# The layer norm of two MLP stages on ScalarE, with a bias that GpSimd forms

## The chip, the cores and the metric

The kernel runs on one core of one Trainium2 chip. A core has TensorE (matmuls, and transposes as matmuls), VectorE, ScalarE and GpSimd, each with its own queue of instructions that it works off in order; the queues meet only in semaphores. The metric is the device time of one execution in microseconds (us); the time of a kernel is the median of its runs.

## The reference, cut to what matters

Input are 64 sequences of 128 tokens with 128 channels. Three transformer layers (self attention, cross attention, MLP) and a final block are applied. The change touches the MLP of the second and third layer, which the kernel calls layers 1 and 2. For each token, with `mu` and `var` over its 128 channels:

```
def _ln(x):
    mu = jnp.mean(x, axis=-1, keepdims=True)
    var = jnp.var(x, axis=-1, keepdims=True)
    return (x - mu) * jax.lax.rsqrt(var + LN_EPS)
...
x_norm2 = modulate(_ln(x), shift_m, scale_m)
h = jax.nn.gelu(x_norm2 @ W_mlp1 + b_mlp1)
h = h @ W_mlp2 + b_mlp2
x = x + gate_m[:, None] * h
```

`modulate(t, shift, sc)` is `t * (1 + sc) + shift`, with one shift and scale per sequence and channel. The hidden width is 512.

## The kernel before

`build` runs the stages one after the other, with a barrier between them: setup, two attention stages of layer 0, its MLP, then for layers 1 and 2 a `packed_attention_layer` and `mlp_phase(nc, r, layer)`, then `refine_phase`. The tokens x stay in SBUF (`r.x`, in the profile `x_res`) for the whole kernel.

`mlp_phase` works on 16 groups of G = 4 sequences, 512 tokens each, and writes one queue for each engine. In all of them `body(g, ...)` is one group's turn and has four chunks c = 0 to 3 of 128 hidden channels. The turns are written out, with no loop at run time. `swiglu` is true for layer 0 only. The steps of one group in layers 1 and 2, with the lines of the profile:

1. VectorE: statistics (`ln_stats`, L1743), mean and variance `mv` (L1750), `vareps` = var + 1e-6 (L1753).
2. GpSimd: `rstd` = vareps to the power -0.5 (`rstd_of`, L1706), 128x4: one value for each token of four sequences.
3. VectorE: `xn` = (x - mean) * rstd (`ln_apply`, L1759), four instructions of 128x128.
4. TensorE: transposes xn into PSUM `l` (L1872). ScalarE: scale and shift give `hT` (`modulate`, L1823). VectorE splits it into a high part (cast, L1766) and a rest (L1768), as the matmuls are done in three products of rounded parts.
5. TensorE: for each chunk three matmuls into PSUM `u` (L299 to L301). ScalarE: gelu to `hid` (L1857). VectorE: high part of it (cast, L1807). The rest is subtracted by GpSimd for chunks 0 to 2 (L1734) and by VectorE for chunk 3 (L1813).
6. TensorE: three matmuls into `y` for each chunk. ScalarE: gate (`apply_gate`, L1834), four instructions. TensorE: transposes back (`mlp_r<-mlp_pg`, L1912). VectorE: adds into x (L1788).

These steps are spread over several turns. In turn g, TensorE's queue has for each chunk c the matmuls `up(g, c)`, then `down` of a chunk three places earlier; behind those of chunk 0 the transposes of xn for group g+1, behind those of chunk 1 the transposes of pg for group g-2. VectorE's queue adds into x of group g-2 at chunk 1, makes the statistics of group g+2 at chunks 0 and 1, splits hT of group g+1 at chunk 2, and, behind the cast of chunk 2, applies the layer norm of group g+2. GpSimd forms rstd of group g+2 ahead of the subtraction of chunk 1. ScalarE has a gelu in each chunk, two `modulate` instructions for group g+1 behind those of chunks 0 and 1, two gates for group g-1 behind those of chunks 2 and 3. `xn`, `rstd` and `mv` have one buffer each.

`after(engine, sem, value)` is a wait that is left out for values that are always met, `wait_ge` a wait, `then_inc` the signal at an instruction's end.

Of the kernel before, what the change touches and what calls it, by code (L numbers as in the profile page):

```python
# [33 lines left out]
G = 4  # L34
# [1604 lines left out]
def mlp_phase(nc, r, layer):  # L1639
# [13 lines left out]
    with nc.cleanup_on_exit(), ExitStack() as ctx:  # L1653
# [8 lines left out]
        def sem(name):  # L1662
            return nc.alloc_semaphore(tag + name)

        w1, w2 = sb("w1", [C, 2, W1], F32R), sb("w2", [C, 2, NC * C], F32R)
        stats, mv = sb("stats", [T, G, 6]), sb("mv", [T, G, 2])
        vareps, rstd = sb("vareps", [T, G]), sb("rstd", [T, G])
        xn, hT = sb("xn", [T, G, C]), sb("hT", [C, GT])
        hT2 = sb("hT2", [C, 2, 2, GT], F32R)
        half = sb("half", [C, 2, GT]) if swiglu else None  # L1670
# [7 lines left out]
        s_xT, s_hT, s_hhi, s_hlo, s_pg, s_pgps, s_x = (  # L1678
            sem(n) for n in ("xT", "hT", "hhi", "hlo", "pg", "pgps", "x"))
        s_w, s_zeroed = sem("w"), sem("zeroed")  # L1680

        s_up, s_half, s_hid, s_hi, s_lo, s_down = (sem(n) for n in ("up", "half", "hid", "hi", "lo", "down"))
        block = ctx.enter_context(nc.Block())
# [18 lines left out]
        @block.gpsimd  # L1702
        def _(pool):
            def rstd_of(g):
                pool.wait_ge(s_var, g + 1)
                nc.gpsimd.tensor_tensor(rstd[:, :], vareps[:, :], r.neg_half[:, :], ALU.pow).then_inc(s_rstd, 1)  # L1706

            def prologue():
                rstd_of(0)
                rstd_of(1)  # L1710
                if layer == 0:

                    nc.gpsimd.memset(r.zero[:, :, :], 0.0).then_inc(s_zeroed, 1)
                    nc.gpsimd.memset(r.slab[:, :], 0.0).then_inc(s_zeroed, 1)
                    for q in range(2 * 4):
                        pool.wait_ge(s_zeroed, 2 + q)
                        nc.gpsimd.affine_select(
                            out=r.slab[:, :], in_=r.slab[:, :], compare_op=ALU.not_equal, fill=1.0,
                            base=-(16 * q + 3), pattern=[[-4, 4]], channel_multiplier=1).then_inc(s_zeroed, 1)
                    pool.wait_ge(s_zeroed, 10)  # L1720
                    for buf in range(3):
                        nc.gpsimd.tensor_copy(
                            r.kp[:, buf, :, :], r.slab[:, :].rearrange("c (g k) -> c g k", k=1).broadcast_to([C, 4, GT])
                            ).then_inc(s_zeroed, 1)

            def body(g, par, late, work, add, nxt, nxt2):
                for c in range(NC if work else 0):
                    n = NC * g + c
                    if c == 1 and nxt2:
                        rstd_of(g + 2)  # L1730
                    if swiglu or c < NC - 1:
                        pool.wait_ge(s_hi, n + 1)

                        nc.gpsimd.tensor_tensor(hid2[:, c, 1, :], hid[:, c % NB, :], hid2[:, c, 0, :].bitcast(F32),  # L1734
                                                ALU.subtract).then_inc(s_lo, 1)

            iterations(pool, body, prologue)

        @block.vector
        def _(dve):  # L1740
# [4 lines left out]
                    last.then_inc(s_stats, 1)  # L1745

            def ln_variance(g):
                after_alone(dve, s_stats, g + 1)
                for b in range(G):
                    last = nc.vector.bn_aggr(mv[:, b, :], stats[:, b, :])  # L1750
# [2 lines left out]
                nc.vector.tensor_scalar(vareps[:, :], mv[:, :, 1], 1e-6, None, ALU.add).then_inc(s_var, 1)  # L1753

            def ln_apply(g):
                after(dve, s_xT, g)
                dve.wait_ge(s_rstd, g + 1)
                for b in range(G):
# [57 lines left out]

        @block.scalar
        def _(act):
            def modulate(g, bs):
                after(act, s_hlo, g)  # L1820
                after_alone(act, s_xT, g + 1)
# [19 lines left out]
            def body(g, par, late, work, add, nxt, nxt2):  # L1841
                for c in range(NC):
# [17 lines left out]
                        modulate(g + 1, [2 * c, 2 * c + 1])  # L1860
                    if c >= 2 and late:
                        apply_gate(g - 1, 1 - par, [2 * c - 4, 2 * c - 3])

            iterations(act, body, lambda: modulate(0, range(G)))

        @block.tensor
        def _(pe):
# [726 lines left out]
```

## Time and profile before

| | us |
|---|---|
| median of 3 runs | 3640.77 (3635.32 to 3642.21) |
| the profiled execution | 3631.1 |
| its span, first to last instruction | 3629.3 |
| MLP of layer 1 in it, about | 2215.9 to 2364.8 |
| MLP of layer 2 in it, about | 3071.1 to 3220.2 |

The profile is of one execution. Its page gives busy times of the engines over the span; the other views used here are the timeline (instructions in order of time, neighbours of one kind merged), groups of instructions by line, and a table of busy times in a stretch. `PE` is TensorE, `PEld` its weight loads, `DVE` VectorE, `ACT` ScalarE, `POOL` GpSimd. Names such as `mlp_xn<-x_res` say what is written and read, without the number of the layer. Times within the profile are set against its own 3631.1 us, which lies 0.27% below the median.

### The profile page before, as it was taken

The numbers are of one execution on the slowest core, as the hardware profiler recorded it, in microseconds if no ns is written. First come the engines' busy times: TensorE is split into PE (matmuls) and PEld (weight loads), VectorE is DVE, ScalarE is ACT, GpSimd is POOL, SyncE is SP. The second block draws the span as 40 slices with busy tenths as digits, with TensorE's granted clock in tenths as the row PEclk, the third lists the DMA queues.
The fourth block names the chain that finished last, engine by engine and source line by source line (L and its number), as shares of the span: only waits on it lengthen the run. The fifth ranks groups of instructions, "written<-read, shape, count | busy, mean of one in ns | idle before, by whom it ended". The sixth has DMA issues, their size and how long they took to land. (4 is left out here: it accounts for less than half of the span.)

```text
span 3629.3 us, 94366 instructions
## 1 busy us (share of the span) xinstructions
PE 3103.4 (86%) x31983; PEld 2065.1 (57%) x31983; DVE 2810.7 (77%) x12664; ACT 2171.0 (60%) x5124; POOL 1200.7 (33%) x1534
## 2 busy tenths in 40 slices
PE   3999967777777769789999997879999998879999
PEld 2454534444444437556666664646666665558887
DVE  5677759999999978578887766858887774966665
ACT  1566645555555647557776665637776664646665
POOL 2000026666666656521122213531112211532221
PEclk9999978889888879889999987969999996979999
DMA  4000000000000000034444430024444441000000
GB/s 130 12 13 13 13 9 8 8 8 9 6 8 8 6 2 1 21 97 107 106 106 104 105 82 3 1 76 106 106 108 100 104 104 29 1 23 10 13 13 16
DMA packets 135426, 162.87 MB, mean 45 GB/s; under 512 B 40742, under 2 KB 85414, under 8 KB 134566
## 3 DMA queue, kind: packets, MB, share of 16 engines
q1 hardware_dynamic: 114182, 121.62, 13.5%
q0 software_dynamic: 12160, 26.04, 3.1%
q10 hardware_dynamic: 8608, 9.18, 1.0%
q8 instruction: 261, 4.28, 0.5%
q14 instruction: 215, 1.76, 0.2%
HBM read 13.81 MB, written 4.19 MB: 5 GB/s over the span
## 5 line engine op out<-in xcount | busy, mean ns | idle before, releaser
L1253 ACT ACTIVATE attn_pT<-attn_t 128x512 f32<-128x512 f32 (+1 forms) x1024 | 555.5, 596 | 335.4 <-PE attn_t L1509 334.6
L1370 DVE TENSOR_REDUCE attn_mx<-attn_s 128x4 f32<-128x512 f32 (+1 forms) x1024 | 549.6, 579 | 152.8 <-PE attn_s L1494 151.3
L636 ACT ACTIVATE topk_prob<-topk_s,topk_nmx 128x77 f32<-128x77 f32 x1024 | 248.3, 326 | 319.7 <-POOL topk_nmx L532 213.2
L1494 PEld LDWEIGHTS attn_s<-packed_keys,packed_queries 32*128 32x128 f32 x4096 | 282.9, 193 | 164.1 <-DVE attn_mx L1370 97.1
L1175 POOL DMA_DIRECT2D packed_queries<-attn_om x256 | 142.7, 557 | 662.9 <-ACT attn_om L1246 659.2
L1494 PE MATMUL attn_s<-packed_keys,packed_queries 32*128 32x128 f32 (+1 forms) x4096 | 348.4, 291 | 14.3 <-DVE attn_mx L1370 6.2
L1534 PE MATMUL attn_o<-attn_pT,attn_vp 128*18 128x128 f32 (+1 forms) x8192 | 336.5, 284 | 0.0
L538 POOL TENSOR_SCALAR topk_mask<-topk_work 128x308 f32<-128x308 f32 x256 | 252.9, 988 | 224.5 <-DVE topk_work L779 222.5
L1509 PE MATMUL attn_t<-packed_queries,packed_keys 32*128 32x128 f32 (+1 forms) x4096 | 306.0, 268 | 1.8 <-ACT attn_pT L1253 1.8
L927 PE MATMUL topk_t<-ident,topk_prob 128*77 128x128 f32 x1024 | 187.3, 313 | 138.5 <-POOL topk_prob L542 138.1
L927 PEld LDWEIGHTS topk_t<-ident,topk_prob 128*77 128x77 f32 x1024 | 139.7, 171 | 250.3 <-issue 140.7
L917 PE MATMUL topk_s<-kbd,topk_qT 128*128 128x308 f32 x512 | 220.9, 517 | 47.4 <-ACT topk_prob L636 43.3
L1734 POOL TENSOR_TENSOR mlp_hid<-mlp_hid 128x512 fp32r<-128x512 f32 x160 | 209.7, 1311 | 156.1 <-DVE mlp_hid L1807 107.9
L1509 PEld LDWEIGHTS attn_t<-packed_queries,packed_keys 32*128 32x128 f32 (+1 forms) x4096 | 232.5, 169 | 6.8 <-ACT attn_pT L1253 4.4
L774 DVE MATCH_REPLACE8 topk_work<-topk_top,topk_s 128x77 f32<-128x77 f32 x1024 | 222.9, 235 | 0.0
L1534 PEld LDWEIGHTS attn_o<-attn_pT,attn_vp 128*18 128x18 f32 (+1 forms) x8192 | 185.2, 99 | 64.5 <-issue 46.2
L542 POOL TENSOR_TENSOR topk_prob<-topk_prob,topk_mask 128x308 f32<-128x308 f32 x256 | 213.5, 834 | 21.3
L779 DVE MATCH_REPLACE8 topk_work<-topk_top,topk_work 128x77 f32<-128x77 f32 x1024 | 218.3, 231 | 0.0
L1554 PE MATMUL attn_l<-packed_keys 128*128 128x512 f32 x576 | 209.0, 454 | 0.8 <-DVE attn_vp L1360 0.7
L763 DVE MAX8 topk_top<-topk_s 128x8 f32<-128x77 f32 x1024 | 172.7, 235 | 23.0 <-PE topk_s L917 23.0
L768 DVE MAX8 topk_top<-topk_work 128x8 f32<-128x77 f32 x1024 | 165.8, 228 | 0.0
L1171 POOL TENSOR_TENSOR attn_rstd<-attn_vareps,neg_half 128x4 f32<-128x4 f32 x64 | 65.8, 1029 | 293.4 <-DVE attn_vareps L1328 293.3
(309 smaller groups left out, 7780.0 us busy)
## 6 DMA issues: line engine op xcount, KB each, us to landing
packed_queries<-attn_qT SPq DMA_DIRECT2D x720, 64.0 KB, 2.2
packed_keys<-attn_kT SPq DMA_DIRECT2D x384, 64.0 KB, 2.1
packed_queries<-attn_om POOLq DMA_DIRECT2D x256, 64.0 KB, 2.4
packed_queries<-zero_rows SPq DMA_DIRECT2D x120, 128.0 KB, 2.7
packed_keys<-attn_kT SPq DMA_DIRECT2D x384, 39.0 KB, 2.1
kbd<-window_kT SPq DMA_DIRECT2D x512, 8.0 KB
kbd<-topk_kT SPq DMA_DIRECT2D x512, 4.8 KB
weights<-in_weights ACTq DMA_DIRECT2D x1, 3524.5 KB, 14.6
```

The source lines that it names most:

```text
L538: nc.gpsimd.tensor_scalar(mask[:, u % 2, :], work[:, u % 4, :], NEG / 2, None, ALU.is_le).then_inc(s_mask, 1)
L542: nc.gpsimd.tensor_tensor(prob[:, u % 4, :], prob[:, u % 4, :], mask[:, u % 2, :], ALU.mult).then_inc(s_picked, 1)
L636: last = nc.scalar.activation(prob[:, u % 4, h * keys:(h + 1) * keys], s_ps[:, u % 2, h * keys:(h + 1) * keys], ACT.Exp, scale=SCALE, bias ...
L774: last = nc.vector.match_replace(wk_[u % 4][:, h, :], top[:, u % 2, h, :], sc[:, h, :], NEG)
L779: last = nc.vector.match_replace(wk_[c % 4][:, h, :], top2[:, c % 2, h, :], wk_[c % 4][:, h, :], NEG)
L917: last = nc.tensor.matmul(s_ps[:, u % 2, 0:cols], qT[:, par, b * T:(b + 1) * T], r.kbd[:, HU * g:HU * g + HU, b * keys:(b + 1) * keys], st ...
L927: last = nc.tensor.transpose(t_ps[0:rows, c % 2, j * T:(j + 1) * T], prob[:, c % 4, j * rows:(j + 1) * rows], r.ident[:, :])
L1253: nc.scalar.activation(pT[0:keys, c % 2, h, :], t_ps[0:keys, h, :], ACT.Exp, scale=SCALE).then_inc(s_exp, 1)
L1370: nc.vector.tensor_reduce(mx[:, (c // 2) % 2, 2 * k + h, :], sc, AX.X, ALU.max).then_inc(s_max, 1)
L1494: last = nc.tensor.matmul(s_ps[:, h, k * KW:(k + 1) * KW], r.qp[32 * j:32 * j + 32, buf, k, b * T:(b + 1) * T], r.kp[32 * j:32 * j + 32, b ...
L1509: last = nc.tensor.matmul(t_ps[0:keys, h, k * T:(k + 1) * T], r.kp[32 * j:32 * j + 32, buf, k, b * KW:b * KW + keys], r.qp[32 * j:32 * j + ...
L1534: last = nc.tensor.matmul(o_ps[32 * k:32 * k + 18, v * T:(v + 1) * T], vp[0:keys, buf, b, k, v, a, :], pT[0:keys, c % 2, a, k * T:(k + 1) ...
```

## The change

In layers 1 and 2, `xn` is formed by ScalarE as `Identity(rstd * x + nmr)`, with `nmr` = -mean * rstd, one value for each token. GpSimd forms nmr with two more 128x4 instructions behind the power, the second of which waits for the first. VectorE's four instructions of L1759 are gone; layer 0 stays as it was. On ScalarE two of the four stand behind the gates of chunk 2 and two behind those of chunk 3, for group g+2. Three waits protect the single buffers: rstd is not overwritten before the last xn that reads it is done, mv not before nmr is formed, xn not before it is transposed.

```
+        nmr = None if swiglu else sb("nmr", [T, G])
...
+        s_nmr = sem("nmr")
...
         @block.gpsimd
         def _(pool):
             def rstd_of(g):
+                if not swiglu:
+                    after(pool, s_xn, g)
                 pool.wait_ge(s_var, g + 1)
                 nc.gpsimd.tensor_tensor(rstd[:, :], vareps[:, :], r.neg_half[:, :], ALU.pow).then_inc(s_rstd, 1)
+                if not swiglu:
+                    pool.wait_ge(s_rstd, g + 1)
+                    nc.gpsimd.tensor_tensor(nmr[:, :], mv[:, :, 0], rstd[:, :], ALU.mult).then_inc(s_nmr, 1)
+                    pool.wait_ge(s_nmr, 2 * g + 1)
+                    nc.gpsimd.tensor_scalar(nmr[:, :], nmr[:, :], -1.0, None, ALU.mult).then_inc(s_nmr, 1)
...
             def ln_variance(g):
+                if not swiglu:
+                    after(dve, s_nmr, 2 * g)
                 after_alone(dve, s_stats, g + 1)
...
             def ln_apply(g):
+                if not swiglu:
+                    return
                 after(dve, s_xT, g)
...
         @block.scalar
         def _(act):
+            def ln_apply(g, bs):
+                if swiglu:
+                    return
+                if bs[0] == 0:
+                    after(act, s_xT, g)
+                    act.wait_ge(s_nmr, 2 * g + 2)
+                for b in bs:
+                    last = nc.scalar.activation(xn[:, b:b + 1, :], r.x[:, G * g + b:G * g + b + 1, :], ACT.Identity,
+                                                scale=rstd[:, b:b + 1], bias=nmr[:, b:b + 1])
+                if bs[-1] == G - 1:
+                    last.then_inc(s_xn, 1)
+
...
                     if c >= 2 and late:
                         apply_gate(g - 1, 1 - par, [2 * c - 4, 2 * c - 3])
-
-            iterations(act, body, lambda: modulate(0, range(G)))
+                    if c >= 2 and nxt2:
+                        ln_apply(g + 2, [2 * c - 4, 2 * c - 3])
+
+            def prologue():
+                ln_apply(0, range(G))
+                modulate(0, range(G))
+                ln_apply(1, range(G))
+
+            iterations(act, body, prologue)
```

The order of the instructions on ScalarE, layer 1, chunks 2, 3 and 0 of one turn and the next, before (L1857 is the gelu, L1834 the gate, L1823 scale and shift):

```order
L1857 ACTIVATE mlp1_hid<-mlp1_u,bias_cols 128x512
L1834 ACTIVATE mlp1_pg<-mlp1_y,gate_bias,mod 128x128 x2
L1857 ACTIVATE mlp1_hid<-mlp1_u,bias_cols 128x512
L1834 ACTIVATE mlp1_pg<-mlp1_y,gate_bias,mod 128x128 x2
L1857 ACTIVATE mlp1_hid<-mlp1_u,bias_cols 128x512
L1823 ACTIVATE mlp1_hT<-mlp1_l,mod 128x128 x2
```

And after, where L1883 is the gelu, L1860 the gate, L1849 scale and shift:

```order
L1883 ACTIVATE mlp1_hid<-mlp1_u,bias_cols 128x512
L1860 ACTIVATE mlp1_pg<-mlp1_y,gate_bias,mod 128x128 x2
L1840 ACTIVATE mlp1_xn<-x_res,mlp1_nmr,mlp1_rstd 128x128 x2
L1883 ACTIVATE mlp1_hid<-mlp1_u,bias_cols 128x512
L1860 ACTIVATE mlp1_pg<-mlp1_y,gate_bias,mod 128x128 x2
L1840 ACTIVATE mlp1_xn<-x_res,mlp1_nmr,mlp1_rstd 128x128 x2
L1883 ACTIVATE mlp1_hid<-mlp1_u,bias_cols 128x512
L1849 ACTIVATE mlp1_hT<-mlp1_l,mod 128x128 x2
```

Between the first and the last xn of a group (L1840) stand a gelu and two gates.

VectorE, layer 1, from the statistics to the rest of chunk 3, before:

```order
L1750 BN_AGGR mlp1_mv<-mlp1_stats 128x2 x4
L1753 TENSOR_SCALAR mlp1_vareps<-mlp1_mv 128x4
L1807 CAST mlp1_hid2<-mlp1_hid 128x512
L1766 CAST mlp1_hT2<-mlp1_hT 128x512
L1768 TENSOR_TENSOR mlp1_hT2<-mlp1_hT,mlp1_hT2 128x512
L1807 CAST mlp1_hid2<-mlp1_hid 128x512
L1759 TENSOR_SCALAR mlp1_xn<-x_res,mlp1_mv,mlp1_rstd 128x128 x4
L1807 CAST mlp1_hid2<-mlp1_hid 128x512
L1813 TENSOR_TENSOR mlp1_hid2<-mlp1_hid,mlp1_hid2 128x512
```

After:

```order
L1762 BN_AGGR mlp1_mv<-mlp1_stats 128x2 x4
L1765 TENSOR_SCALAR mlp1_vareps<-mlp1_mv 128x4
L1821 CAST mlp1_hid2<-mlp1_hid 128x512
L1780 CAST mlp1_hT2<-mlp1_hT 128x512
L1782 TENSOR_TENSOR mlp1_hT2<-mlp1_hT,mlp1_hT2 128x512
L1821 CAST mlp1_hid2<-mlp1_hid 128x512 x2
L1827 TENSOR_TENSOR mlp1_hid2<-mlp1_hid,mlp1_hid2 128x512
```

The four instructions between the casts of chunks 2 and 3 are gone; nothing else moved there.

## Rows read from the trace of the kernel before

**Rows 1.** The page, part 1: busy us (share of the span) and instructions.

```profile
PE 3103.4 (86%) x31983; PEld 2065.1 (57%) x31983; DVE 2810.7 (77%) x12664; ACT 2171.0 (60%) x5124; POOL 1200.7 (33%) x1534
```

**Rows 2.** Busy us by stretch: ten groups of the MLP of layer 1.

```profile
core 0: us, PE busy (x) PEld busy (x) DVE busy (x) ACT busy (x) POOL busy (x), PEclk, DMA share, GB/s
2258.00:2344.44 86.44, 70.88 (x322) 50.61 (x321) 80.63 (x212) 55.60 (x121) 50.59 (x41) 1.00 0.00 1
```

**Rows 3.** Timeline, TensorE: start us, us, line, [idle before, releaser].

```profile
2268.59 0.63 PE L1872 MATMUL mlp_l<-ident,mlp_xn 128*128 128x128 f32 x4 [1.40 <-DVE mlp_xn L1759]
...
2277.24 0.63 PE L1872 MATMUL mlp_l<-ident,mlp_xn 128*128 128x128 f32 x4 [1.39 <-DVE mlp_xn L1759]
```

**Rows 4.** Timeline, VectorE in that group, and L1759 eight groups on.

```profile
2271.10 0.69 DVE L1788 TENSOR_TENSOR x_res<-mlp_r,x_res 128x512 f32<-128x512 f32 x1 [0.48 <-PE mlp_r L1912]
...
2272.53 0.42 DVE L1766 CAST mlp_hT<-mlp_hT 128x512 fp32r<-128x512 f32 x1
2272.98 0.69 DVE L1768 TENSOR_TENSOR mlp_hT<-mlp_hT 128x512 fp32r<-128x512 f32 x1
2273.59 1.52 DVE L1807 CAST mlp_hid<-mlp_hid 128x512 fp32r<-128x512 f32 x1
2275.03 2.06 DVE L1759 TENSOR_SCALAR mlp_xn<-x_res,mlp_mv,mlp_rstd 128x128 f32<-128x128 f32 x4
...
2344.16 2.06 DVE L1759 TENSOR_SCALAR mlp_xn<-x_res,mlp_mv,mlp_rstd 128x128 f32<-128x128 f32 x4
```

**Rows 5.** Timeline, start of the MLP of layer 1.

```profile
2218.68 1.11 DVE L1759 TENSOR_SCALAR mlp_xn<-x_res,mlp_mv,mlp_rstd 128x128 f32<-128x128 f32 x4 [0.20 <-POOL mlp_rstd L1706]
...
2219.85 1.12 PE L1872 MATMUL mlp_l<-ident,mlp_xn 128*128 128x128 f32 x4 [5.65 <-DVE mlp_xn L1759]
...
2221.00 1.50 ACT L1823 ACTIVATE mlp_hT<-mlp_l,mod 128x128 f32<-128x128 f32 x4 [7.97 <-PE mlp_l L1872]
...
2222.49 1.12 DVE L1759 TENSOR_SCALAR mlp_xn<-x_res,mlp_mv,mlp_rstd 128x128 f32<-128x128 f32 x4 [0.25 <-POOL mlp_rstd L1706]
...
2223.52 0.42 DVE L1766 CAST mlp_hT<-mlp_hT 128x512 fp32r<-128x512 f32 x1
```

**Rows 6.** Timeline, GpSimd in the group of rows 3.

```profile
2272.36 1.12 POOL L1706 TENSOR_TENSOR mlp_rstd<-mlp_vareps,neg_half 128x4 f32<-128x4 f32 x1 [0.38 <-DVE mlp_vareps L1753]
2273.45 1.37 POOL L1734 TENSOR_TENSOR mlp_hid<-mlp_hid 128x512 fp32r<-128x512 f32 x1
2275.19 1.31 POOL L1734 TENSOR_TENSOR mlp_hid<-mlp_hid 128x512 fp32r<-128x512 f32 x1 [0.36 <-DVE mlp_hid L1807]
```

**Rows 7.** Small GpSimd instructions of other stages: two groups (busy, mean ns), then timeline.

```profile
L532 POOL TENSOR_SCALAR topk_nmx<-topk_top 128x4 f32<-128x4 f32 x256 | 58.1, 227 | 41.6 <-DVE topk_top L763 20.5
...
L2054 POOL TENSOR_TENSOR refine_w1s<-refine_weights,refine_w1s 128x256 fp32r<-128x256 f32 x1 | 0.7, 722 | 0.0
...
1519.95 1.01 POOL L1171 TENSOR_TENSOR attn_rstd<-attn_vareps,neg_half 128x4 f32<-128x4 f32 x1 [1.62 <-DVE attn_vareps L1328]
...
800.24 0.98 POOL L538 TENSOR_SCALAR topk_mask<-topk_work 128x308 f32<-128x308 f32 x1 [0.61 <-DVE topk_work L779]
801.30 0.84 POOL L542 TENSOR_TENSOR topk_prob<-topk_prob,topk_mask 128x308 f32<-128x308 f32 x1
802.22 0.23 POOL L532 TENSOR_SCALAR topk_nmx<-topk_top 128x4 f32<-128x4 f32 x1
802.57 0.33 ACT L636 ACTIVATE topk_prob<-topk_s,topk_nmx 128x77 f32<-128x77 f32 x1 [1.24 <-POOL topk_nmx L532]
```

**Rows 8.** Timeline, ScalarE in the group of rows 3.

```profile
2272.56 0.81 ACT L1834 ACTIVATE mlp_pg<-mlp_y,gate_bias,mod 128x128 f32<-128x128 f32 x2
2273.26 0.69 ACT L1857 ACTIVATE mlp_hid<-mlp_u,bias_cols 128x512 f32<-128x512 f32 x1
2273.85 0.80 ACT L1834 ACTIVATE mlp_pg<-mlp_y,gate_bias,mod 128x128 f32<-128x128 f32 x2
```

**Rows 9.** Timeline, end of the MLP of layer 1, ScalarE to TensorE.

```profile
2361.83 1.50 ACT L1834 ACTIVATE mlp_pg<-mlp_y,gate_bias,mod 128x128 f32<-128x128 f32 x4 [2.74 <-PE mlp_y L301]
...
2363.48 0.63 PE L1912 MATMUL mlp_r<-ident,mlp_pg 128*128 128x128 f32 x4 [1.75 <-ACT mlp_pg L1834]
```

## The prediction, made before the changed kernel ran

> **What bounds the kernel now.** Read the page first. No engine is at its limit over the whole span: TensorE is busy 86%, VectorE 77%, ScalarE 60%, GpSimd 33% [rows 1]. The page averages over eight stages, and the change touches two of them, the MLP of layer 1 and of layer 2, about 150 us each. So the next view is the table of busy time over a stretch of the layer 1 MLP that holds ten groups: 86.44 us, of which TensorE is busy 70.88, VectorE 80.63, ScalarE 55.60 and GpSimd 50.59, at a granted clock of 1.00 [rows 2]. VectorE looks like the bound, but its busy time holds waiting.
>
> The timeline shows what closes the loop. One group takes 8.65 us, from one block of L1872 transposes (xn to PSUM) to the next, 2268.59 to 2277.24, and before the second the TensorE sat idle 1.39 us for L1759 on VectorE [rows 3]. I follow that period back.
> - From the transposes at 2268.59, TensorE goes on through six matmuls, the transposes of pg, and VectorE can add into x at 2271.10 (L1788): **2.51 us** [rows 3, 4].
> - From there VectorE is busy without a gap to the end of L1759, 2275.03 + 2.06 = 2277.09: **5.99 us** [rows 4].
> - VectorE's end to the next transposes: 2277.24 - 2277.09 = **0.15 us**.
>
> The sum, 2.51 + 5.99 + 0.15 = 8.65, is the period. L1759 starts at 2275.03 and again, eight groups on, at 2344.16 [rows 4], 8.64 us each. Two rows of it are swollen: the cast L1807 takes 1.52 us where L1766, a cast of the same shape, takes 0.42, and the four L1759 take 2.06 us against 1.11 to 1.12 at the start of the stage [rows 4, 5]. Both run while GpSimd's subtractions L1734 run (2273.45 + 1.37 = 2274.82; the next begins at 2275.19) [rows 4, 6].
>
> **What the change removes from the loop.** The four L1759 (2.06 us) go, and so does VectorE's part of the loop behind the small statistics: nothing of the next xn waits any more for L1766, L1768 and the blocked L1807. What stays of the 5.99 us is L1788 to the start of GpSimd's pow L1706: 2272.36 - 2271.10 = 1.26 us. The rest, 5.99 - 1.26 = 4.73 us, is replaced.
>
> **What it puts in.** Now xn depends on pow, multiply, negate (GpSimd), then on ScalarE. In order:
> - pow, as before: 1.12 us [rows 6]. Until now it lay beside VectorE's work; now it is in the loop.
> - multiply, 128x4, tensor by tensor: no such row exists. Below: GpSimd's 128x512 takes 1.31 us and its 128x256 takes 0.72 us [rows 6, 7], 0.59 us for 256 columns, so a line through them leaves 0.14 us for four columns. Above: pow itself has this shape and takes 1.01 us when VectorE leaves it alone [rows 7]. I take 0.20, near the line and near the 0.23 us of a GpSimd TENSOR_SCALAR of 128x4 [rows 7], since a multiply is what the wide rows are made of and a power is not.
> - negate: 0.23 us, that same row.
> - two gaps, as each of the two waits for the end of the one before: L542 waits for L538 in that way and starts 801.30 - 801.22 = 0.08 us behind it [rows 7]. I take 0.10 each.
> - GpSimd to ScalarE: 802.57 - 802.45 = 0.12 us [rows 7].
> - ScalarE's stretch from the first to the last xn. The new order there is two xn, gelu, two gates, two xn (the order rows of the change). Two L1834 hold ScalarE for 2273.26 - 2272.56 = 0.70 us, so 0.35 each, and a gelu for 2273.85 - 2273.26 = 0.59 us, while the last one counts whole, 0.46 us [rows 8]. Sum: 5 x 0.35 + 0.59 + 0.46 = 2.80 us.
> - ScalarE to TensorE: 2363.48 - (2361.83 + 1.50) = 0.15 us [rows 9].
>
> The new loop: 2.51 + 1.26 + 1.12 + (0.10 + 0.20 + 0.10 + 0.23) + 0.12 + 2.80 + 0.15 = **8.59 us** against 8.65. So 3.6 us of saved and unblocked VectorE work buys 0.06 us per group: the gain is handed to a chain of the same length on other engines. The three prices in the brackets have 0.63 us; the period is as before when they have 0.69.
>
> Is anything else late before that? ScalarE's load rises by 4 x 0.35 us, from 5.5 busy to about 7 of 8.6: not the bound, but its gelu of chunk 3 now stands behind two xn that wait for GpSimd. That gelu would start at 2273.48 + 0.63 + 0.12 + 0.70 = 2274.93 instead of 2273.26 [rows 8]; it feeds the cast of chunk 3, L1813 and matmuls that stand behind the next transposes and add, so I cost it at nothing. The subtraction L1734 of chunk 1 stands on GpSimd behind the two new instructions, 0.63 us later; the matmuls of L299 that wait for it end a microsecond before the transposes (TensorE's idle 1.39 us [rows 3] is the cover), so nothing either, as long as the bracket stays under about 1.5 us. The added waits that only protect a buffer (s_xn on GpSimd, s_nmr on VectorE, s_xT on ScalarE) were met a whole half-group before.
>
> **The start of each stage.** Before, the first transposes are at 2219.85; the ScalarE part ends at 2221.00 + 1.50 = 2222.50, but the cast L1766 waits until 2223.52, behind the second L1759 [rows 5]. The first L1759 starts at 2218.68, 0.03 us behind pow, and 2219.85 - 2218.65 = 1.20 us pass from pow to the transposes. After, they are 0.63 + 0.12 + (3 x 0.35 + 0.46) + 0.15 = 2.41 us, 1.2 us later. The wait behind L1759 hid 1.0 of that, so 0.2 us is lost, 0.4 us in both layers. The second xn on ScalarE and the table load behind it fit before the first gelu.
>
> **The sum.** Twelve full periods in each layer: 24 x (8.59 - 8.65) = -1.4 us; start +0.4 us; total -1.0 us. The profiled execution took 3631.1 us (span 3629.3), so it would be 3630.1. The median of the runs shown is 3640.8, 0.27% above it; a change of one microsecond moves both alike: **3639.8 us**. A measurement of this kernel can tell about 0.2%, 7.3 us, from no change; that is 0.30 us per group over 24 groups, so everything between periods of 8.35 and 8.95 us reads as the same.
>
> **The rivals.**
> *Slower, the read port.* In the loop the multiply would start at 2273.48 + 0.10 = 2273.58. VectorE's L1768 runs until 2273.67 and the cast L1807 would run from 2273.59 to 2274.01, now unblocked [rows 4, 6]. If GpSimd's small operations can read only when VectorE is through with both, the multiply ends near 2274.2 and the negate near 2274.5, a bracket of 1.0 us: period 8.96, 24 x 0.31 + 0.4 = +7.8 us, **3648.6 us**. It is slower from a bracket of 0.69 us on. For it: pow takes 1.12 us here and 1.01 us where VectorE is idle [rows 6, 7], and VectorE's own cast was held until GpSimd ended. Against it: pow lost only 0.11 us although three VectorE instructions passed beside it, and they lost nothing [rows 4, 6]. The Trainium skill, SBUF — State Buffer, "Who interferes with whom", says that a cast in the two-port mode and GpSimd exclude each other for the whole instruction, whoever issues first, and that a VectorE instruction with two SBUF inputs keeps out GpSimd's reads. By that rule this rival is the likely one if the cast is issued first, and the 1.52 us cast agrees; the pow row speaks for short conflicts only.
>
> *Slower, dearer pieces.* The multiply costs like pow, 1.01 us: period 9.40, +18 us + 0.4, **3659 us**. Or an xn on ScalarE, reading SBUF instead of PSUM with two pointer operands, takes up its whole 0.46 us without overlap: three intervals, +0.33 us, period 8.92, +6.9 us, 3647.7 us. For PSUM sources the rows show the overlap; for this source none does.
> By the Trainium skill, ScalarE: Activation LUTs, "What ACT_TABLE_LOAD costs", an ACTIVATE has a fixed cost, 0.093 us for each pointer operand and 0.833 ns per element, and back to back they overlap; worked out, an estimate, 0.39 us apart instead of the 0.35 us of the rows [rows 8]. With three xn intervals the loop would be 0.12 us longer. The rows decide, and its result stays within no change.
>
> *Faster, cheap pieces.* Multiply 0.14 as on the line, negate 0.20 and gaps of 0.06 make the bracket 0.46 us and the period 8.42: 24 x (-0.23) + 0.4 = -5.1 us, 3635.7 us. With 0.33 instead of 0.35 us between ScalarE's instructions it is 8.32, -7.5 us, **3633.3 us**. A larger gain needs xn to leave the loop altogether; TensorE's busy time would then allow 7.1 us and less. The in-order queue of TensorE, in which the transposes stand before the matmuls that the next add into x needs, forbids it.
>
> **How the numbers follow.** Forecast, period 8.42 to 8.85: 0.66. The port: 0.17. Dearer pieces: 0.06. Cheap pieces: 0.11. The port rival lies right at the bound, so I count three quarters of it as slower; with the dearer pieces that is 0.19. The cheap case reaches 7.3 us only at its far end; with the scatter of the runs and an error of my chain itself I count 0.09 as faster. Same: 0.72. The range takes in the cheap end and the port rival with a microsecond of scatter, 3633 to 3650, and leaves out the dear multiply and the tails.
>
> **What would show it.** In the profile after: L1840 (the four xn on ScalarE) as what TensorE's transposes wait for, in place of L1759; the period between blocks of transposes within 0.2 us of 8.65; ScalarE idle before the first xn of a group, ended by GpSimd's negate; the two GpSimd instructions at 0.2 us each; the cast at 0.42 us in chunk 2, where it now stands as L1821 and meets no subtraction (the one of chunk 3 may be the blocked one instead, at no cost); VectorE's busy time in the stretch of ten groups down from 80.6 us by the ten times 2.06 of L1759, to about 60. I am wrong if the multiply or the negate is much over 0.3 us, if the xn on ScalarE are more than 0.4 us apart, or if the transposes wait for something that is no part of this chain.

## Result, and the profile after

| | before | after |
|---|---|---|
| median, us | 3639.03 (3634.42 to 3642.21, 5 runs) | 3654.18 (3649.85 to 3663.13, 5 runs) |
| profiled execution, us | 3631.1 | 3649.85 |

The ratio is 1.0053, 95% interval [1.0032, 1.0075]. I forecast no change, 3639.8 us with a range to 3650; the kernel became slower by about 15 us (12 to 27 us by the interval). Times and ratios below leave out two executions, one of e9 (5060 us) and one of e16 (4350 us), in which the granted clock was 0.66 and 0.64 instead of about 0.92 over the whole execution.

The page of after, part 1, beside [rows 1]:

```profile
PE 3115.8 (85%) x31983; PEld 2072.8 (57%) x31983; DVE 2742.8 (75%) x12536; ACT 2221.2 (61%) x5252; POOL 1217.0 (33%) x1598
```

VectorE gave up 68 us and ScalarE took on 50 us, as meant. Ten groups of the layer 1 MLP of after, busy us by stretch, columns as in [rows 2]:

```profile
2246.76:2340.82 94.06, 75.40 (x321) 54.10 (x320) 57.60 (x171) 70.75 (x160) 55.50 (x60) 0.95 0.00 1
```

Three things stand there. Ten groups take 94.06 us instead of 86.44. VectorE's busy time is down from 80.63 to 57.60, close to the 60 that I expected. And the granted clock reads 0.95, where before it was 1.00: something that the prediction does not speak of.

The starts of GpSimd's pow (L1706 before, L1711 after; 16 in each stage) give every period. Before, the eleven from the fifth pow on are all 8.63 to 8.65 us in layer 1. After, in layer 1: 8.92, 8.93, 8.94, **10.51**, 8.94, 8.93, 8.93, **10.53**, **10.50**, 8.93, 8.93, 8.94; in layer 2 five of twelve are 10.4 to 10.7. So there are two losses: 0.28 us in every group, and 1.5 to 1.8 us more in eight of the 24. Here is one ordinary group, timeline of after (start us, us, engine, line, [idle before, releaser]):

```profile
2284.62 0.69 DVE L1782 TENSOR_TENSOR mlp_hT<-mlp_hT 128x512 fp32r<-128x512 f32 x1
2285.23 0.48 POOL L1714 TENSOR_TENSOR mlp_nmr<-mlp_mv,mlp_rstd 128x4 f32<-128x4 f32 x1
2285.23 0.42 DVE L1821 CAST mlp_hid<-mlp_hid 128x512 fp32r<-128x512 f32 x1
2285.80 0.23 POOL L1716 TENSOR_SCALAR mlp_nmr<-mlp_nmr 128x4 f32<-128x4 f32 x1
2286.12 0.88 ACT L1840 ACTIVATE mlp_xn<-x_res,mlp_nmr,mlp_rstd 128x128 f32<-128x128 f32 x2 [1.11 <-POOL mlp_nmr L1716]
2287.31 0.50 PE L299 MATMUL mlp_y<-mlp_hid,mlp_w 128*128 128x512 f32 x1 [0.96 <-POOL mlp_hid L1744]
2288.16 0.87 ACT L1840 ACTIVATE mlp_xn<-x_res,mlp_nmr,mlp_rstd 128x128 f32<-128x128 f32 x2
2289.17 0.63 PE L1905 MATMUL mlp_l<-ident,mlp_xn 128*128 128x128 f32 x4 [0.91 <-ACT mlp_xn L1840]
2291.68 0.69 DVE L1802 TENSOR_TENSOR x_res<-mlp_r,x_res 128x512 f32<-128x512 f32 x1 [1.06 <-PE mlp_r L1945]
2292.69 0.17 DVE L1765 TENSOR_SCALAR mlp_vareps<-mlp_mv 128x4 f32<-128x4 f32 x1
2293.00 1.09 POOL L1711 TENSOR_TENSOR mlp_rstd<-mlp_vareps,neg_half 128x4 f32<-128x4 f32 x1 [1.03 <-DVE mlp_vareps L1765]
```

The loop is the one of the prediction: the transposes L1905 (in place of L1872, [rows 3]) wait for ScalarE's L1840, ScalarE for the negate L1716, GpSimd for vareps, VectorE for the transposes of pg. The multiply L1714, however, takes 0.48 us and starts in the same hundredth as VectorE's cast L1821. At the start of the stage, where no cast of this kind stands beside it, the same instruction takes 0.20 us (timeline of after, GpSimd; the negate behind it takes 0.25):

```profile
2227.79 0.20 POOL L1714 TENSOR_TENSOR mlp_nmr<-mlp_mv,mlp_rstd 128x4 f32<-128x4 f32 x1
```

The long groups are another matter. Stretches of after in layer 1 (columns as above, so the granted clock is the third number from the end):

```profile
2310.00:2315.00 5.00, 4.04 (x16) 2.48 (x14) 2.92 (x11) 3.58 (x9) 3.97 (x5) 1.00 0.00 0
2315.00:2320.00 5.00, 4.11 (x16) 3.37 (x16) 2.38 (x7) 3.60 (x9) 1.58 (x2) 0.66 0.00 0
2320.00:2325.00 5.00, 4.04 (x18) 2.74 (x17) 2.86 (x11) 3.06 (x7) 3.45 (x5) 1.00 0.00 0
```

and TensorE's own timeline in the second of them and just behind it:

```profile
2315.98 0.84 PE L1905 MATMUL mlp_l<-ident,mlp_xn 128*128 128x128 f32 x4 [0.89 <-ACT mlp_xn L1840]
2317.05 0.63 PE L300 MATMUL mlp_u<-mlp_hT,mlp_w 128*128 128x512 f32 x1
2317.48 0.63 PE L301 MATMUL mlp_u<-mlp_hT,mlp_w 128*128 128x512 f32 x1
...
2320.09 0.39 PE L300 MATMUL mlp_u<-mlp_hT,mlp_w 128*128 128x512 f32 x1
2320.32 0.40 PE L301 MATMUL mlp_u<-mlp_hT,mlp_w 128*128 128x512 f32 x1
```

From the transposes on, matmuls start 0.43 us apart (2317.05 to 2317.48); three microseconds later it is 0.23 again (2320.09 to 2320.32). In between TensorE works at the lower level of its clock, 1.2 GHz, for some four microseconds; the 0.66 of the stretch is a mean of 1.00 and 0.50. In both kernels the stage begins at the lower level, as the stage ahead of it ended (granted clock 0.50 until about 2228 before and 2238 after). From there to the last group the kernel before stays at 1.00.

Where the time went: between the first and the last pow the two stages grew by 132.11 - 123.98 = 8.1 and 135.17 - 124.23 = 10.9 us, 19.1 together. The eight low-clock groups hold 12.8 of these, the longer period nearly all of the rest (24 x 0.28 = 6.7). Ahead of the two stretches, between them and behind them the two profiled executions differ by +9.1, -10.3 and +0.6 us, which add up to nearly nothing. So the profiled executions differ by 19 us, the medians by 15.

### The profile page after: what moved, and what is told of

Same layout as the page of the kernel before. It is cut to its first block and busy times, and to the rows that moved or that the text cites. A ratio compares the mean times of both kernels' runs of the same rounds, so it can differ in the third digit from the quotient of the medians.

```text
span 3647.8 us, 94490 instructions
## 1 busy us (share of the span) xinstructions
PE 3115.8 (85%) x31983; PEld 2072.8 (57%) x31983; DVE 2742.8 (75%) x12536; ACT 2221.2 (61%) x5252; POOL 1217.0 (33%) x1598
## 5 line engine op out<-in xcount | busy, mean ns | idle before, releaser
L622 ACT COPY topk_pT<-topk_t 77x512 f32<-77x512 f32 x256 | 150.3, 587 | 26.8 <-PE topk_t L927 26.2
```

## Experiments

Periods below are the usual distances between the starts of pow at full clock, from the fifth on. The low-clock groups are counted in one profiled execution of each kernel, of 24 groups in the two stages. Each kernel was run beside the kernel before on its own chip, and ratios are against that. The chips differ: the kernel before had medians of 3631.26 us beside e1, e3, e4 and e5, 3634.33 beside e2, e8, e9 and e10, and 3631.02 beside e12, e15 and e16, against 3639.03 in the table above. So kernels are compared by their ratios and not by their microseconds.

| run | period, us | low-clock groups | ratio to before |
|---|---|---|---|
| before | 8.65 | 0 | 1 |
| after | 8.93 | 8 | 1.0053 [1.0032, 1.0075] |
| e1 cast behind multiply | 8.94 | 14 | 1.0074 [1.0061, 1.0088] |
| e8 cast behind negate | 8.65 | 0 | 1.0010 [0.9996, 1.0024] |
| e2 negate first | 8.88 | 11 | 1.0052 [1.0033, 1.0072] |
| e3 six filler matmuls | 8.93 | 0 | 1.0015 [1.0003, 1.0027] |
| e15 three, first gap | 8.93 | 0 | 1.0011 [0.9991, 1.0030] |
| e16 three, second gap | 8.93 | 0 | 1.0013 [0.9999, 1.0028] |
| e4 before, four aggregations | 8.89 | 0 | 1.0020 [1.0005, 1.0034] |
| e9 before, eight | 9.15 | 0 (e9b) | 1.0039 [1.0022, 1.0055] |
| e5 early variance | 8.41 | 1 | 0.9988 [0.9978, 0.9998] |
| e10 before, early variance | 8.85 | 0 | 1.0014 [0.9996, 1.0032] |
| e12 variance in chunk 0 | 8.71 | about 10 | 1.0013 [0.9998, 1.0028] |

### The multiply and the cast

```
                         dve.wait_ge(s_hid, n + 1)
+                        if c == 2 and nxt2:
+                            dve.wait_ge(s_nmr, 2 * (g + 2) + 1)
                         nc.vector.tensor_copy(hid2[:, c, 0, :], hid[:, c % NB, :]).then_inc(s_hi, 1)
```

> After, with one added wait on VectorE: the cast L1821 of chunk 2, which starts in the same moment as GpSimd's multiply, now waits until the multiply has ended. Nothing else is moved. Theory one (the multiply takes 0.48 us and not 0.20 because the cast runs beside it): the multiply falls to 0.20 us, the negate stays at 0.23 if the cast no longer meets a small instruction, and the period at full clock goes from 8.93 to 8.93 - 0.28 = 8.65 us; 24 x (-0.28) = -6.7 us, 3647.5 us if the clock drops stay. Rival (the multiply is slow for itself, for instance behind a pow): it stays at 0.48 us and the period at 8.93 us, 3654 us. Third way: the conflict moves on to the negate, which then takes about 0.48 us, and nothing is gained.

Measured: 3657.19 us, and the third way. One group of that run, timeline:

```profile
2299.89 0.20 POOL L1714 TENSOR_TENSOR mlp_nmr<-mlp_mv,mlp_rstd 128x4 f32<-128x4 f32 x1
2300.18 0.51 POOL L1716 TENSOR_SCALAR mlp_nmr<-mlp_nmr 128x4 f32<-128x4 f32 x1
2300.22 0.43 DVE L1823 CAST mlp_hid<-mlp_hid 128x512 fp32r<-128x512 f32 x1 [0.25 <-PE mlp_y L301]
```

The multiply is back to 0.20 us, and the negate behind it, which had taken 0.23, takes 0.51. Whichever small instruction stands beside the cast is held for about 0.28 us; that it is "slow for itself" is excluded. The multiply still begins beside the end of VectorE's L1782 in this run and takes its 0.20 us, so in after it was the cast that held it. So the next run took the cast out of both, the same edit with `2 * (g + 2) + 2`:

> As the run with the cast behind the multiply, where the conflict only moved on to the negate (0.51 us beside the cast, and the multiply down to 0.20), but now the cast of chunk 2 waits for the negate too. Theory: both small instructions run alone, 0.20 and 0.23 us, and the period falls from 8.93 by 0.28 to 8.65 us; against the after kernel -6.7 us and fewer groups at the low clock, 3636 to 3648 us. Rival: the cast is now issued together with GpSimd's subtraction of chunk 1 and one of them is held for the other's whole length, about 1.3 us; if the subtraction is the one held, TensorE's matmul L299 that waits for it (0.96 us idle) becomes later, and the period stays or grows: 8.9 to 9.2 us, 3655 us or more.

Measured: 3638.90 us, timeline of one group:

```profile
2282.52 0.20 POOL L1714 TENSOR_TENSOR mlp_nmr<-mlp_mv,mlp_rstd 128x4 f32<-128x4 f32 x1
2282.81 0.23 POOL L1716 TENSOR_SCALAR mlp_nmr<-mlp_nmr 128x4 f32<-128x4 f32 x1
2283.00 1.28 POOL L1744 TENSOR_TENSOR mlp_hid<-mlp_hid 128x512 fp32r<-128x512 f32 x1
2283.13 0.88 ACT L1842 ACTIVATE mlp_xn<-x_res,mlp_nmr,mlp_rstd 128x128 f32<-128x128 f32 x2 [0.84 <-POOL mlp_nmr L1716]
2283.17 3.03 DVE L1823 CAST mlp_hid<-mlp_hid 128x512 fp32r<-128x512 f32 x2 [0.56 <-POOL mlp_nmr L1716]
2284.33 0.51 PE L299 MATMUL mlp_y<-mlp_hid,mlp_w 128*128 128x512 f32 x1 [0.68 <-POOL mlp_hid L1744]
2286.19 0.63 PE L1907 MATMUL mlp_l<-ident,mlp_xn 128*128 128x128 f32 x4 [0.88 <-ACT mlp_xn L1842]
```

The cast starts 0.17 us behind the subtraction, and now it is VectorE that is held: two casts in 3.03 us, each of them beside a subtraction. Nobody waits for them in this loop; the matmul L299 comes earlier, not later (idle 0.68 instead of 0.96). The period is 8.65 us, and the low-clock groups are gone with it. With this one wait the changed kernel does what I had predicted for the change alone: its ratio to before is 1.0010, no change.

The negation was also moved out of the chain to the front, as a negated mean that GpSimd forms before pow (`nm = -mv`, then pow, then `nmr = nm * rstd`):

> After, with GpSimd's negation moved out of the chain: it negates the mean as soon as the aggregation is there, beside VectorE's vareps, and ahead of pow; behind pow only the multiply is left. Removed from the chain are the negate and its gap, 0.23 + 0.09 = 0.32 us; pow starts later by what the negate (0.23 us) outlasts vareps (0.17 us) and a gap, some 0.15 us. Theory (the chain through GpSimd and ScalarE closes the loop): the period goes from 8.93 to about 8.93 - 0.32 + 0.15 = 8.76 us, -4 us, and fewer groups at the low clock, between 3636 and 3650 us. Rival (the loop closes elsewhere): 8.93 us stays.

Measured: 3658.07 us, period 8.88, timeline:

```profile
2281.99 0.43 DVE L1825 CAST mlp_hid<-mlp_hid 128x512 fp32r<-128x512 f32 x1
2282.06 0.73 POOL L1714 TENSOR_SCALAR mlp_nm<-mlp_mv 128x4 f32<-128x4 f32 x1 [0.87 <-DVE mlp_mv L1766]
2282.33 0.42 DVE L1784 CAST mlp_hT<-mlp_hT 128x512 fp32r<-128x512 f32 x1
2282.47 1.38 POOL L1716 TENSOR_TENSOR mlp_rstd<-mlp_vareps,neg_half 128x4 f32<-128x4 f32 x1
2283.93 0.20 POOL L1720 TENSOR_TENSOR mlp_nmr<-mlp_nm,mlp_rstd 128x4 f32<-128x4 f32 x1
```

A miss: the negate now meets two casts and takes 0.73 us. Pow is listed from 2282.47, while the negate runs to 2282.79, so its 1.38 us hold 0.3 us of the same waiting. Of the 0.17 us that I expected 0.05 came, and the clock still falls in 11 groups.

### The clock

Six matmuls a group, whose product is overwritten, in TensorE's two gaps of after (behind the up product of chunk 0, and before the transposes):

```
+            def filler(g, par):
+                pe.wait_ge(s_hT, g + 1)
+                for _ in range(3):
+                    nc.tensor.matmul(l_ps[:, :], w1[:, 0, 0:C], hT2[:, par, 0, :], start=True, stop=True)
...
                     if work:
                         up(g, c, par)
+                    if c == 0 and nxt and work and late and not swiglu:
+                        filler(g, par)
...
                     if c == 0 and nxt and work:
+                        if late and not swiglu:
+                            filler(g, par)
                         transpose_xn(g + 1)
```

> After, with six matmuls more in every group of layers 1 and 2 that compute nothing of use (a product into the PSUM tile of xn's transposes, which overwrite it): three in the gap before the first matmul of the second-last down product, three in the gap before the transposes of xn. Both gaps are idle time of TensorE, 0.96 and 0.91 us, and three matmuls take 3 x 0.23 = 0.70 us, so they should delay nothing. Theory one (the drops of the granted clock in the two stages, nine groups of about 10.5 us instead of 8.93, come with TensorE's idle time in the longer loop, and cost 9 x 1.6 = 14 us by themselves): no five-microsecond window of the two stages under 0.95, all periods at 8.93 us or a little more, 3654 - 14 = 3640 us. Rival (the drops have nothing to do with what TensorE does in these gaps): they stay, 3654 us or more.

Measured: 3636.13 us, every period from the fifth pow on 8.93 to 8.95 us except for 8.77 and 9.21 in layer 2. (The expectation counts nine low-clock groups in after; between the first and the last pow there are eight.) A stretch of layer 1 (TensorE, its weight loads, VectorE, ScalarE, GpSimd, granted clock); layer 2 reads 1.00 as well:

```profile
2240.00:2300.00 60.00, 56.92 (x254) 41.54 (x253) 38.98 (x116) 47.66 (x109) 38.55 (x42) 1.00 0.00 1
```

TensorE does more and the kernel is faster: the distance to after, 1.0053 to 1.0015, is 0.38% or 14 us (between 5 and 23 us with both intervals), all from the clock, since the period did not move. The traces say it more closely: its stages (first to last pow) take 127.4 and 127.5 us, against 132.1 and 135.2 of after, which is 12.3 us. Then only one of the two gaps was filled:

> After, with three idle matmuls in each group instead of six, in the gap before the down product (L299, 0.96 us idle), so that 0.3 us of it is left, and the gap of 0.91 us before the transposes stays: 1.14 us idle a group in all. Theory (the low clock needs both gaps, since before has one of 1.40 us and never drops): all groups at 8.93 us, as with six, 3636 to 3641 us. Rival (either gap alone is enough): groups of 10.5 us remain, about half as many.

> The mirror of the run with three matmuls in the first gap: three in the gap before the transposes of xn (0.91 us idle, 0.2 us left), and the gap of 0.96 us before the down product stays. Theory (the low clock needs both gaps): all groups at 8.93 us, 3636 to 3641 us. Rival: groups of 10.5 us remain.

Measured: 3634.12 and 3636.17 us; all groups are at full clock in both. Three matmuls in either gap are enough. The gaps left, timeline of TensorE, first e15, then e16:

```profile
2282.11 0.50 PE L299 MATMUL mlp_y<-mlp_hid,mlp_w 128*128 128x512 f32 x1 [0.29 <-POOL mlp_hid L1744]
2283.95 0.63 PE L1905 MATMUL mlp_l<-ident,mlp_xn 128*128 128x128 f32 x4 [0.87 <-ACT mlp_xn L1840]
```

```profile
2280.45 0.50 PE L299 MATMUL mlp_y<-mlp_hid,mlp_w 128*128 128x512 f32 x1 [0.96 <-POOL mlp_hid L1744]
2282.32 0.63 PE L1905 MATMUL mlp_l<-ident,mlp_xn 128*128 128x128 f32 x4 [0.20 <-ACT mlp_xn L1840]
```

Is it simply that a longer loop leaves TensorE too idle? Then before, made longer, must drop too. Four more aggregations on VectorE, into a spare tile, then eight:

```
+                if not swiglu:
+                    for b in range(G):
+                        nc.vector.bn_aggr(spare[:, b, :], stats[:, b, :])
                 for b in range(G):
                     last = nc.vector.bn_aggr(mv[:, b, :], stats[:, b, :])
```

> The kernel before, with four more of VectorE's aggregations (L1750 of before) in each group of layers 1 and 2, written to a spare tile, between the add into x and vareps. They lengthen the loop of before by 0.30 us (four of them stand 0.40 us apart from the next row, the last counted whole), so the period goes from 8.65 to 8.95 us, about that of after, with nothing of the change in it. Theory one (the clock drops come with a loop of this length, in which TensorE is idle more): drops like those of after, 24 x 0.30 + 14 = +21 us, 3660 us. Rival (the drops belong to the changed order of work and not to the length of the loop): the clock stays at 1.00 in the two stages, +7.2 us, 3646 us.

> The kernel before, with eight more of VectorE's aggregations in each group instead of four; four of them gave a period of 8.89 us, 0.25 us over 8.65, and the clock stayed at 1.00. So the period here is 8.65 + 0.50 = 9.15 us, longer than that of after at full clock (8.93), and TensorE idles more than there: 9.15 - 7.09 = 2.06 us a group against 1.84. Theory one (the drops come with the sum of TensorE's idle time, and the run with four was just short of it): low-clock groups appear, before + 12 + up to 14 us. Theory two (they come with the way in which after spreads its idle time, 0.96 and 0.91 us two microseconds apart, where before has one gap of 1.40 us): none appear, before + 12 us.

> The same kernel as the one with eight more aggregations, looked at once more, since the profiled execution of that run was a disturbed one. The period should be 9.15 us again in all groups. If the drops of the granted clock come with the sum of TensorE's idle time, windows with a low clock appear among groups 3 to 14; if not, all windows read 1.00.

Measured: 3639.94, 3652.1 and 3645.26 us (the last is one execution). The granted clock is 1.00 in e4, and in e9b from the third group to the last of both stages. A stretch of e9b in layer 1, and TensorE's gaps in one of its groups:

```profile
2240.00:2300.00 60.00, 47.37 (x211) 1.00 0.00 1
```

```profile
2279.70 0.47 PE L299 MATMUL mlp_u<-mlp_hT,mlp_w 128*128 128x512 f32 x1 [0.49 <-ACT mlp_hid L1861]
2280.79 0.50 PE L299 MATMUL mlp_y<-mlp_hid,mlp_w 128*128 128x512 f32 x1 [0.17 <-POOL mlp_hid L1735]
2283.15 0.63 PE L1876 MATMUL mlp_l<-ident,mlp_xn 128*128 128x128 f32 x4 [1.40 <-DVE mlp_xn L1763]
```

With a period of 9.15 us, longer than that of after, and 2.06 us of idle time against 1.87, no group drops; the loss is the plain 24 x 0.5 = 12 us, within its interval (8 to 20 us). The sum of idle time is not the cause. What the traces list beside it is where the idle time lies. After, e1 and e2 each have two gaps of 0.8 to 1.05 us within two microseconds of each other, and drop. Where one of the two is filled (e3, e15, e16), or the first is 0.68 us (e8), nothing drops, and nothing drops with one gap of 1.40 us and the small ones further off (before, e4, e9b). e12, below, drops right behind single gaps of 2 us, and e5 drops once, in the one group in which its second gap was 1.18 us instead of 0.90 (timelines of e12 and of e5):

```profile
2279.43 0.47 PE L299 MATMUL mlp_y<-mlp_hid,mlp_w 128*128 128x512 f32 x1 [2.04 <-POOL mlp_hid L1744]
...
2282.47 1.05 PE L1905 MATMUL mlp_l<-ident,mlp_xn 128*128 128x128 f32 x4
```

```profile
3173.52 0.50 PE L299 MATMUL mlp_y<-mlp_hid,mlp_w 128*128 128x512 f32 x1 [0.60 <-POOL mlp_hid L1744]
3175.66 0.74 PE L1907 MATMUL mlp_l<-ident,mlp_xn 128*128 128x128 f32 x4 [1.18 <-ACT mlp_xn L1842]
```

The pattern is narrow, though, and no rule. e10, below, has gaps of 1.19 and 0.75 us in nearly every group, 2.4 us apart and 1.94 us together, more than after has, and never drops (timeline):

```profile
2282.26 0.47 PE L299 MATMUL mlp_u<-mlp_hT,mlp_w 128*128 128x512 f32 x1 [1.19 <-issue]
2284.65 0.52 PE L1874 MATMUL mlp_l<-ident,mlp_xn 128*128 128x128 f32 x3 [0.75 <-DVE mlp_xn L1759]
```

One group of e8 has 0.69 and 1.16 us (ahead of the matmuls at 3182.96 and 3185.09 us), together more than the group of e5 that drops and as far apart, and keeps its clock. What is shown is that filling either gap of after keeps the clock, and that a longer loop by itself doesn't lose it. That idle time close together is what costs it is argued from the list, and no run tests it by moving a gap alone. By the Trainium skill, TensorE: Matmul & The Clock Gate, "A second HAM failure mode: psum-queue depth-cycling", frequent short idling between groups of matmuls can make the clock swing between its two levels. The traces agree: in after the granted clock reads 1.00 and 0.66 by turns with no gap over 0.96 us in such a group of layer 1. Why eight groups of after drop and sixteen with nearly the same gaps don't stays open.

### The variance ahead of the add

In after the statistics of a later group stand behind the add into x, although they don't need it. Moved ahead of it:

```
+                    if work and nxt2 and c == 1 and not swiglu:
+                        ln_variance(g + 2)
                     if add and c == 1:
                         after_alone(dve, s_pgps, g - 1)
...
-                    if nxt2 and c == 1:
+                    if nxt2 and c == 1 and swiglu:
                         ln_variance(g + 2)
```

> After, with VectorE's variance of the group after next (aggregation and vareps) moved ahead of its add into x, so that pow, multiply and negate no longer stand behind the transposes of pg. In the trace of after vareps could be ready at 2291.1 instead of 2292.86, GpSimd's subtraction of chunk 0 ends at 2291.97, so pow would start at about 2292.0 instead of 2293.0, a microsecond earlier; ScalarE waited 1.11 us for the negate before its first xn. Theory one (the loop runs through this chain): the period falls by 0.6 to 1.0 us, to 7.9 to 8.3, and with it the clock drops go, since TensorE idles less: 3654 - 24 x 0.6 - 14 = 3625 us or less. Rival (the chain is not what closes the loop, or VectorE's later work becomes late instead): the period stays within 0.1 of 8.93, 3652 to 3656 us.

Measured: 3626.86 us, period 8.41, one low-clock group: 0.12% under before (interval 0.02 to 0.22%), 0.65% under after. The period fell short of the 7.9 to 8.3 us that I expected. Rows of its trace show what may be a part of it, timeline:

```profile
2282.44 0.69 DVE L1782 TENSOR_TENSOR mlp_hT<-mlp_hT 128x512 fp32r<-128x512 f32 x1
2282.53 0.67 POOL L1714 TENSOR_TENSOR mlp_nmr<-mlp_mv,mlp_rstd 128x4 f32<-128x4 f32 x1
```

The multiply now starts 0.09 us behind VectorE's subtraction of two SBUF tiles and ends 0.07 us behind its end: 0.67 us instead of 0.20, in 23 of 24 groups. No run takes that meeting away. The same move in the kernel before:

> The kernel before, with the same move that took 27 us off after: the variance of the group after next ahead of the add into x. Theory (the move pays only once xn has left VectorE): the aggregation fills 0.37 us of the 0.48 us in which VectorE waits for the transposes of pg, but vareps then meets GpSimd's subtraction of chunk 0 and is held until that ends, as in the after kernel with the move (1.07 us instead of 0.17), and the add starts about 0.9 us later; the other VectorE work of the loop still stands behind it. Period 8.65 - 0.48 + 0.9 = 9.07 us, +10 us against before. Rival (the move is good by itself): the period falls by up to 0.48 us to 8.17, -11 us.

Measured: 3635.96 us, period 8.85 instead of 8.65. The add starts 3.33 us behind the transposes instead of 2.51, so it loses 0.82 of the 0.9 us; from there to the end of xn it is 5.37 instead of 5.99 us, where I had counted on 0.48 us less. The held row is as foreseen in both kernels, here e5 and then e10, timeline:

```profile
2279.83 1.28 POOL L1744 TENSOR_TENSOR mlp_hid<-mlp_hid 128x512 fp32r<-128x512 f32 x1 [2.20 <-DVE mlp_hid L1823]
2280.08 1.07 DVE L1765 TENSOR_SCALAR mlp_vareps<-mlp_mv 128x4 f32<-128x4 f32 x1
2281.29 1.16 POOL L1711 TENSOR_TENSOR mlp_rstd<-mlp_vareps,neg_half 128x4 f32<-128x4 f32 x1 [0.17 <-DVE mlp_vareps L1765]
```

```profile
2287.00 1.07 DVE L1753 TENSOR_SCALAR mlp_vareps<-mlp_mv 128x4 f32<-128x4 f32 x1
```

VectorE's vareps takes 1.07 us instead of 0.17 beside the subtraction in both. In e5 the period falls all the same, as xn has left VectorE; in e10 it grows. One step further, with variance and pow in chunk 0:

> After, with the variance of the group after next directly behind its statistics in chunk 0 (in the earlier run it stood in chunk 1, behind the cast of chunk 0), and with GpSimd's pow, multiply and negate ahead of its subtraction of chunk 0 instead of that of chunk 1. In the trace of the earlier run the statistics end at 2279.42, so vareps would end at 2279.9, before GpSimd has a subtraction that could hold it (1.07 us there), and pow would start at 2279.97 instead of 2281.29; multiply and negate end near 2281.9, the first xn can follow ScalarE's gate at 2283.05 without its wait of 0.58 us. Theory: the period falls by up to that wait, from 8.41 to 7.83 us, 24 x (-0.58) = -14 us against 3627, 3613 us. Rival: GpSimd's three subtractions, now all behind the small instructions, become late for TensorE or hold VectorE's casts, and the period stays within 0.1 of 8.41, 3625 to 3629 us.

Measured: 3638.62 us, period 8.71 and, in most of the low-clock groups, 9.46 or more: a miss for both theories. GpSimd's subtractions became late, and TensorE waits for them in one piece of about 2 us, the one shown above: in 90 us of that run (groups by line) the down product L299 has 12.1 us of idle time in front of it.

```profile
L299 PE MATMUL mlp_y<-mlp_hid,mlp_w 128*128 128x512 f32 x40 | 17.5, 437 | 12.1 <-POOL mlp_hid L1744 12.1
```

## Why the prediction was wrong

Two steps failed. The granted clock was taken to stay at 1.00, and the later subtraction of chunk 1 was costed at nothing: the clock took 12.8 of the 19.1 us by which the two stages grew. And the bracket of multiply, negate and their gaps was taken at 0.63 us where it measured 0.88: with ScalarE's stretch, 0.11 us too short in the sum, it makes the period 8.93 us, and that is nearly all of the rest. With the longer period and the clock kept (e3, e15, e16) the ratio is 1.0011 to 1.0015, some 5 us, so it was the clock that took the time out of my range.

- **The loop was right.** Transposes, pg, add, vareps, pow, multiply, negate, ScalarE, transposes: each releaser in the group above is the one named. The sum with after's rows is 2.51 (2289.17 to 2291.68) + 1.32 (to pow at 2293.00) + 1.08 + 0.88 (bracket) + 0.10 + 2.91 (2286.12 to 2288.16 + 0.87) + 0.14 = 8.94 us, against 8.93 measured.
- **The bracket was mis-sized, 0.88 us instead of 0.63.** Both prices, 0.20 and 0.23 us, were right where nothing of VectorE stands beside them (e8), and the gaps were 0.08 and 0.09 us; the step that failed was to take them undisturbed. A multiply much over 0.3 us is one of the signs of being wrong that I had named. I had seen the cast standing where the multiply would start, and gave that 17 in 100 because pow loses only 0.11 us in such company. The row that spoke for it was the other one, the cast held for a whole subtraction [rows 4]. The rival put the bracket at 1.0 us, the period at 8.96 and the time at 3648.6 us; its mechanism came true for the cast, a little smaller (0.88, 8.93), and the price of the clock was in no rival. By the Trainium skill, SBUF — State Buffer, "Who interferes with whom", such a cast and GpSimd exclude each other whoever comes first, and the order of issue decides who waits. Both sides can be held, as e1 and e8 show, 0.51 instead of 0.23 us for the negate and 3.03 us for two casts. The order is less plain: in e8 the instruction listed first went through, but in e1 the negate that was held is listed 0.04 us ahead of the cast, so starts this close do not tell it.
- **ScalarE's stretch was 2.91 instead of 2.80 us.** Two xn take 0.88 us and the second of a pair starts 0.39 to 0.40 us behind the first, not 0.35 as for PSUM sources [rows 8]. The estimate worked out from the Trainium skill, ScalarE: Activation LUTs, "What ACT_TABLE_LOAD costs", was 0.39. The trace agrees, with 0.39 to 0.40. I had let the PSUM rows decide.
- **The clock was missing altogether**, 12.8 us in the traces, two thirds of what the stages lost. I read 1.00 in [rows 2] and took it as given. A longer loop alone did not change it (e4, e9b); what changed is that the wait of 0.16 us for GpSimd's subtraction became 0.96 us, since the subtraction of chunk 1 stands behind the two small instructions. I costed that delay at nothing, because TensorE's idle time covers it. It does cover it, but one gap of 1.40 us became two, 0.96 and 0.91 us. With either of the two filled the clock stays (e15, e16); why some groups drop and others don't is open.
- **The casts and buffers were right.** The chunk 2 cast takes 0.42 us again, the one of chunk 3 is the held one, VectorE's load fell as computed, and no protecting wait shows up in the full turns (GpSimd's second pow of each stage waits for the first xn, but stands 3.52 us behind the first pow where it was 3.76 before).
- **The start of a stage was right.** From pow's end to the first transposes it is 2.36 us (2227.71 to 2230.07) against my 2.41.
- **A slip without effect.** The "3.6 us of saved and unblocked VectorE work" counts the whole cast. Unblocked are 1.52 - 0.42 = 1.10 us, so it is 3.2 us; the sum doesn't use it.
- **e8 bears out the sum**: with the conflict removed, the period is 8.65 against my 8.59, most of the rest is ScalarE's stretch, and the clock stays.

## What to carry to other kernels

When small instructions of GpSimd are put into a loop's chain, look which VectorE instructions stand at that moment. In these runs such a meeting cost one of the two up to the other's remaining time, and one wait that let the cast go later was cheaper than the meeting. When a change moves or splits an idle gap of TensorE, ask what its clock will do even if nothing is late; a few idle matmuls in one gap are a cheap test of it. Taking work off an engine can need a second edit to pay: here the work moved off VectorE was worth 0.12% once the statistics had been moved ahead of the add, while that second edit alone was worth nothing in the kernel before (1.0014).

## What I had not expected of the hardware

- In layer 1 of after the granted clock fell to 1.2 GHz for about four microseconds at a time, with no gap over 0.96 us in the loop, and stayed at 2.4 GHz with a gap of 1.40 us and more idle time in all (e9b), and with gaps of 1.19 and 0.75 us (e10).
- Three 128x512 matmuls a group that compute nothing of use took 12.4 us off the two stages (127.4 + 127.5 us in e15 and in e16 against 132.1 + 135.2).
- A GpSimd instruction on 128x4 values, 0.20 us of work, waited for a 128x512 cast as a big one does; with two casts in its way one took 0.73 us (e2), and beside a subtraction of VectorE 0.67 us (e5).
